# Moving five value products out of a graph layer's prologue, with GpSimd sharing the sort's ranks

## The chip, the cores and the metric

The kernel runs on one core of a Trainium2 chip. The metric is the device time in microseconds (us) of one execution, as a median of several. A profile is one further execution that the hardware profiler recorded.

## What is computed

One layer of a graph network over 1250 nodes of 512 features and 40000 edges, followed by a routed mixture of eight experts. Cut to what the change touches:

```python
xn = _layernorm(x, axis=-1)
xs = xn[:, :C] @ (W_in2f_s / np.sqrt(C))                # node table, with xv: 4 products of 128 features
sj, vj = xs[idx_j], xv[idx_j]                           # gathered for every edge
h = shifted_softplus(f_ij @ Wf1 + bf1)                  # filter network over the edges
W = (h @ Wf2 + bf2) * rcut_ij[:, None]
agg = segment_sum(x_ij, idx_i)                          # messages made of sj, vj and W, summed by node
q, k, v = xn @ Wq, xn @ Wk, xn @ Wv                     # q and k then softmax over each head
context = einsum('bhnd,bhne->bhde', k, v)
out = einsum('bhnd,bhde->bhne', q, context)
x = x + gnn + (out @ Wo + bo)
x = x + ffn(_layernorm(x))                              # top 2 of 8 experts
```

## The kernel before

The nodes form ten tiles of 125 rows (NB = 10, t below). The edges lie as 313 columns of 128 edges. The kernel has a prologue, a filter loop of 79 steps of four columns, a loop over gathered messages, and the experts. Each engine runs its own list of instructions in the order in which the code writes them; semaphores are the only link, so an engine that waits holds up all that is written behind the wait.

*Prologue.* SyncE (SP) loads x, the weights and the features. For each tile VectorE normalises (`normal`), TensorE transposes (`transpose_x`, L2058), ScalarE copies the transposed tile out (`evac_xT`, L1080), TensorE multiplies it with the table weights (`table_product`, L2070) and with Wv (`value_product`, L2081), and ScalarE copies both results (`table_rows`, L1085; `values`, L1092). All ten value products are in the prologue (L2091 and the following lines). SP stores each table tile.

*The sort.* Edges are to be stored in order of the receiving node. VectorE finds each edge's block of 125 nodes (`receiving_blocks`, L1400) and for each of the ten blocks a mask, a running count and a rank (`count_block`, L1411: mask, scan, copy of the last count, product, sum). TensorE sums the counts over the partitions, VectorE makes the bases of the blocks (`block_bases`, L1420) and the place of every edge (`places_in_blocks`, L1439, ten operations). GpSimd then makes the places of six spare columns (`spare_places`, L956) and scatters six empty records (`spare_record`, L938).

*The filter network* has weights that are split into a high and a low part. GpSimd orders them (L918 to L932), ScalarE rounds them, VectorE makes the low parts. Before the loop starts, the first columns must have gone through: features (`stage_f`, `stage_f_low`), TensorE's `transposes` and `layer1`, ScalarE's `radial` and `log_part`, VectorE's `hidden`, then `high` (ScalarE) and `low` (VectorE).

*The filter loop.* In step m TensorE multiplies four columns (`layer2`, L2227; the first instruction of a step is the bias product at L2240), ScalarE copies the first column out (`first_column`, L1202) and VectorE the other three (`column`, L1587), and GpSimd scatters four columns to their places in memory (`scatter`, L953). A ring of four steps holds the results, so that `stage` (L1555) waits for the scatter of four steps before. Beside this the steps carry the attention: from step 3 on, six steps make a group for one tile t (`beside`, L2247), with r = 0 to 5 the step in the group: the query product in r 0 and 1, the key product in r 2 and 3, the transposes of the queries in r 4, the context product in r 5. In the last steps of the first five groups (8, 14, 20, 26, 32) VectorE also runs `run_level` (L1446).

## Time and profile before

| | |
|---|---|
| median of 3 runs | 1272.28 us (1270.4 to 1272.28) |
| the profiled execution | 1271.56 us, span 1269.5 us |
| TensorE busy in the span | 1190.8 us (94%) |
| VectorE busy | 1071.0 us (84%) |
| GpSimd busy | 870.8 us (69%) |
| ScalarE busy | 812.4 us (64%) |
| prologue, until the first filter product | 75.2 us |
| filter loop, first to last start of a scatter | 79.5 to 493.7 us |

The profile page gives each engine's busy time, and groups of instructions by line with the idle time ahead of them and what ended it. The trace of the same execution can be asked for the chain of waits (the work that ended last, followed back), for timelines of one engine, and for stretches. Busy time of TensorE (PE) includes the overlap of pipelined products; PEld is its weight load. L12 is line 12 of the kernel. POOL is GpSimd, DVE is VectorE, ACT is ScalarE. A group such as "x8" in a timeline is so many instructions, and an fp32 product appears as two.

### The profile page before, as it was taken

What the parts mean: (1) busy time and instruction counts of PE and PEld (TensorE: products, weight loads), DVE (VectorE), ACT (ScalarE), POOL (GpSimd) and SP (SyncE); (2) the same over time, 40 slices, a digit from 0 to 9 for tenths busy, and PEclk for the clock granted to TensorE, in tenths of its full rate; (3) what the DMA queues carried; (4) which work ended last, traced back from release to release, by engine and by line L of the source; (5) the groups of instructions that cost most, each with busy time, mean ns of one, the idle gap of its engine ahead of it and who ended that gap; (6) DMA issues with size and microseconds to landing.
All of it is one profiled execution on the core that took longest, in us unless ns stands there. A gap on an engine that the chain in (4) does not pass through costs nothing.

```text
span 1269.5 us, 16249 instructions
## 1 busy us (share of the span) xinstructions
PE 1190.8 (94%) x4108; PEld 700.0 (55%) x4108; DVE 1071.0 (84%) x1998; ACT 812.4 (64%) x1822; POOL 870.8 (69%) x795
## 2 busy tenths in 40 slices
PE   4999999989999999899999999999999999977995
PEld 3566666767766664344444444444444444766882
DVE  5958999899989995699999999999999997589325
ACT  3667777777767660576776767767767674775330
POOL 6357777777777775688888888888888881053650
PEclk8989999999999999899999999999999999987996
DMA  9248876887799966988888898988898881554557
GB/s 276 63 153 298 296 266 256 314 304 270 291 320 358 305 236 233 351 302 309 316 309 307 305 315 305 311 309 302 315 309 304 310 265 34 203 188 143 183 172 235
DMA packets 106608, 337.65 MB, mean 266 GB/s; under 512 B 16783, under 2 KB 17803, under 8 KB 100373
## 3 DMA queue, kind: packets, MB, share of 16 engines
q0 software_dynamic: 57264, 188.75, 41.5%
q1 hardware_dynamic: 49252, 147.88, 35.4%
q8 instruction: 34, 0.56, 0.2%
q14 instruction: 58, 0.47, 0.1%
HBM read 211.27 MB, written 125.30 MB: 265 GB/s over the span
## 4 chain that ended last, share of the span: by engine, by line
PE 76%; DVE 12%; DMA 4%; issue 3%; ACT 2%; POOL 1%; SPq 0%; DVEq 0%; POOLq 0%; ACTq 0%
PE PS L2306 22%; PE PS L2311 22%; PE PS L2242 11%; PE PS L2431 6%; DVE RR L1587 4%; PE PS L2109 3%; PE PS L2119 2%; PE PS L2087 2%; DMA X<-in_x 1%; DMA edge_records<-RR 1%; DVE h_low L1580 1%; PE PS L2240 1%; PE PS L2409 1%; POOL edge_records L953 1%; PE PS L2202 1%
## 5 line engine op out<-in xcount | busy, mean ns | idle before, releaser
L990 POOL DMA_INDIRECT RR<-node_table,RR x322 | 445.4, 1383 | 112.2 <-issue 64.0
L1250 ACT ACTIVATE RR<-RR 128x256 f32<-128x256 f32 x966 | 394.5, 494 | 194.1 <-PE PS L2311 155.6
L953 POOL DMA_INDIRECT edge_records<-RR x316 | 315.0, 997 | 107.3 <-issue 72.7
L2306 PE MATMUL PS<-RR 128*125 128x512 f32 x644 | 291.6, 595 | 3.8 <-DVE RR L1765 3.7
L2311 PE MATMUL PS<-RR 128*125 128x512 f32 x644 | 289.6, 592 | 0.0
L2306 PEld LDWEIGHTS PS<-RR 128*125 128x125 f32 x644 | 121.0, 189 | 162.1 <-issue 144.4
L2311 PEld LDWEIGHTS PS<-RR 128*125 128x125 f32 x644 | 120.9, 188 | 155.5 <-issue 155.5
L1587 DVE TENSOR_TENSOR RR<-PS,RR 128x512 f32<-128x512 f32 x237 | 161.0, 687 | 23.4 <-PE PS L2242 22.7
L2242 PE MATMUL PS<-wf_high,h_high 128*128 128x512 f32 x316 | 148.5, 470 | 8.7 <-DVE RR L1587 8.4
L1765 DVE TENSOR_TENSOR RR<-RR 128x1536 f32<-128x1536 f32 (+1 forms) x81 | 141.0, 1741 | 0.0
L2242 PE MATMUL PS<-wf_low,h_high 128*128 128x512 f32 x316 | 125.9, 398 | 0.0
L2242 PE MATMUL PS<-wf_high,h_low 128*128 128x512 f32 x316 | 125.9, 398 | 0.0
L1736 DVE TENSOR_TENSOR RR<-RR 128x1024 f32<-128x1024 f32 (+1 forms) x81 | 98.2, 1213 | 21.6 <-DMA RR<-node_table,RR 21.5
L1748 DVE TENSOR_SCALAR RR<-iota_f,RR 128x125 f32<-128x125 f32 x322 | 109.6, 343 | 0.0
L1195 ACT ACTIVATE h_high<-RR 128x512 fp32r<-128x512 f32 x79 | 49.8, 630 | 55.1 <-PE PS L2242 52.0
L2242 PEld LDWEIGHTS PS<-wf_high,h_high 128*128 128x128 f32 x316 | 60.4, 191 | 27.6 <-DVE RR L1587 12.2
L1202 ACT ACTIVATE RR<-PS 128x512 f32<-128x512 f32 x79 | 47.2, 597 | 40.7 <-PE PS L2242 40.7
L1754 DVE TENSOR_TENSOR RR<-RR 128x512 f32<-128x512 f32 (+1 forms) x81 | 55.4, 684 | 20.4 <-ACT RR L1250 20.1
L2242 PEld LDWEIGHTS PS<-wf_low,h_high 128*128 128x128 f32 x316 | 60.7, 192 | 14.0 <-issue 9.1
L2242 PEld LDWEIGHTS PS<-wf_high,h_low 128*128 128x128 f32 x316 | 60.2, 190 | 14.2
L1785 DVE TENSOR_TENSOR RR<-RR,PS 125x1024 f32 x52 | 63.1, 1214 | 4.2 <-PE PS L2311 3.7
L1570 DVE SCALAR_TENSOR_TENSOR RR<-PS,RR 128x512 f32<-128x512 f32 x79 | 53.9, 683 | 9.5 <-ACT RR L1187 9.3
(354 smaller groups left out, 1799.1 us busy)
## 6 DMA issues: line engine op xcount, KB each, us to landing
RR<-edge_records SPq DMA_DIRECT2D x48, 1040.0 KB, 6.6
expert_inputs<-RR SPq DMA_DIRECT2D x8, 2313.0 KB, 17.7
RR<-edge_records SPq DMA_DIRECT2D x27, 520.0 KB, 5.1
RR<-edge_records SPq DMA_DIRECT2D x15, 780.0 KB, 5.5
RR<-in_L_ffn_beta_w SPq DMA_DIRECT2D x8, 1024.0 KB
expert_w_raw<-in_L_ffn_expert_w SPq DMA_DIRECT2D x8, 1024.0 KB, 7.0
RR<-edge_records SPq DMA_DIRECT2D x31, 260.0 KB, 5.2
edge_records<-RR POOLq DMA_INDIRECT x322, 4.3
```

The source lines that it names most:

```text
L953: g.indirect_dma_start(out=rec_dram, out_offset=place, in_=ST[:, j, :], in_offset=None).then_inc(scattered[c], 16)
L990: g.indirect_dma_start(out=GB[q % GBS][:, t, 1:5, :].rearrange("p k n -> p (k n)"), out_offset=None, in_=tab_dram, in_offset=bass.Indirect ...
L1250: last = a.activation(message_slot(q)[:, t, k:k + 5:4, :], GB[q % GBS][:, t, 0:k + 3:k + 2, :], ACT.Copy, scale=record_slot(q)[:, t, 4 * C ...
L1587: v.tensor_tensor(ST[:, c * STEP + j, 0:4 * C], PS[:, w_bank(m, j), :], b2_rows, ALU.add)\
L1736: v.tensor_tensor(gb[:, :, 0:2, :].rearrange("p t k n -> p k t n"), record_slot(q)[:, :, 0:2 * C].rearrange("p t (k n) -> p k t n", k=2), ...
L1748: v.tensor_scalar(OH[q % OHS][:, t, 0:NT], iota_f[:, 0:NT], rec[:, 3:4], rec[:, 5:6], ALU.is_equal, ALU.mult).then_inc(onehot, 1)
L1765: v.tensor_tensor(vec, vec, record_slot(q)[:, :, 2 * C:3 * C].unsqueeze(2).to_broadcast([P, n, 3, C]), ALU.mult).then_inc(d_ready, 1)
L1785: v.tensor_tensor(dst_ap, dst_ap, PS[0:NT, b:b + 2, :].rearrange("p b n -> p (b n)"), ALU.add)\
L2242: last = te.matmul(PS[:, w_bank(m, j), :], part[:, c % 2, edges], weights[:, :, :].rearrange("p k n -> p (k n)"), start=(j > 0 and weights ...
L2306: te.matmul(PS[0:NT, 2 * (r % PSS), :], OH[q % OHS][:, t, 0:NT], GB[q % GBS][:, t, 1:5, :].rearrange("p k n -> p (k n)"), start=(n == 0), ...
L2311: te.matmul(PS[0:NT, 2 * (r % PSS) + 1, :], OH[q % OHS][:, t, 0:NT], message_slot(q)[:, t, 0:4, :].rearrange("p k n -> p (k n)"), start=(n ...
L2431: last = te.matmul(PS[:, 2 + n % 2, :], x[:, n % 2, k, :], w[:, k, :], start=(j == 0), stop=(j == len(terms) - 1))
```

## The change

Value products 5 to 9 leave the prologue. Each becomes four quarters in the last step of a group t = 0 to 4 (`late_value`): two quarters behind the first column, one behind the second, one behind the fourth; its result goes through bank 6, which the queries use too, and ScalarE copies it at the head of the next step. As the memory of Wv is used again by then, Wv is loaded a second time. The first of the four quarters waits until ScalarE has copied the transposed queries out.

GpSimd makes the product and the sum of the ranks of blocks 0 to 7 (`rank_block`), in two buffers each, so VectorE's `count_block` waits from block 2 on for GpSimd's product of two blocks before; blocks 8 and 9 stay with VectorE. Five blocks stand ahead of the ordering of the filter weights on GpSimd, three behind it. Constants that GpSimd made early come behind the spare places. The six empty records are scattered in steps 1 to 6. The first batch of blank rows for the experts (`blank_words`) goes from step 3 to step 11.

SP issues the first filter layer's weights and the first features ahead of Wq and Wk. TensorE sums the counts after tile 4's transposes; tiles 5 to 9 use bank 6 for the transposes and bank 7 for the table. The first filter columns are interleaved with the table products of tiles 5 to 9. VectorE makes the places ahead of the first hidden layer. The inverse edge lengths are made early.

Buffers, groups and steps are renumbered; of the diff stands here what the order of the work depends on.

buffers, banks and steps:

```diff
+        running, block_product, own_ranks = (tA, tB), (tC, tD), (srcf, bkt)
...
+        WV_again = R1[:, sorted_at:sorted_at + KD * D].rearrange("p (k n) -> p k n", k=KD)
+        assert sorted_at + KD * D <= c1.at
...
+        FRONT = 5
...
+        EARLY_XT = 6
+        RANKED = 8
...
+        SPARE_STEPS = range(1, 1 + NCOL - LOOPED)
+        BLANK_STEP = [SPARE_STEPS[-1] + 5] + [2 * CHUNK * k + 2 for k in range(1, BLANKS)]
```

SyncE: loads:

```diff
-            load_projection(WQ, Wq, wqkv_in[0])
-            load_projection(WK, Wk, wqkv_in[1])
-            load_features(0)
-            load_features(1)
...
+            load_features(0)
+            load_projection(WQ, Wq, wqkv_in[0])
+            load_projection(WK, Wk, wqkv_in[1])
+            load_features(1)
...
+            sp.wait_ge(edge_places, 2)
+            load_projection(WV_again, Wv, wqkv_in[2])
```

GpSimd:

```diff
+            def rank_block(t):
+
+                pool.wait_ge(counts_ready, t + 1)
+                g.tensor_tensor(rnk if t == 0 else block_product[t % 2], block_mask[t], running[t % 2], ALU.mult)\
+                    .then_inc(ranked, 1)
+                pool.wait_ge(ranked, multiplied(t))
+                if t:
+                    g.tensor_tensor(rnk, rnk, block_product[t % 2], ALU.add).then_inc(ranked, 1)
+
+            for t in range(5):
+                rank_block(t)
...
+            for t in range(5, RANKED):
+                rank_block(t)
+
+            pool.wait_ge(nrm_inv, 1)
+            g.tensor_tensor(meta[:, 0:RC1, 0:3], rraw, inv.unsqueeze(2).to_broadcast([P, RC1, 3]), ALU.mult)\
+                .then_inc(dirs_ready, 1)
...
-            for n in range(NCOL - LOOPED):
-                spare_record(LOOPED + n)
...
+                if m in SPARE_STEPS:
+                    spare_record(LOOPED + SPARE_STEPS.index(m))
```

ScalarE:

```diff
+            table_rows(2)
+            evac_xT(3)
+            moments_of((6, 7))
+            later_std(slice(6, 8), 7)
+            values(2)
+            table_rows(3)
+            evac_xT(4)
+            rounded_weights()
+            stage_f(0)
+            stage_f(1)
+            moments_of((8, 9))
+            later_std(slice(8, NB), NB - 1)
+            a.preload_act_table_set("natural_log_exp_and_others")
+            values(3)
+            table_rows(4)
+            evac_xT(5)
+            act.wait_ge(w_ordered, 2)
+            a.activation(b2hl[0:2, :], b2f, ACT.Copy).then_inc(w_rounded, 1)
 
             def radial(i, c):
...
+                if r == 0 and 1 <= t <= NB - FRONT:
+                    values(FRONT + t - 1)
...
-            bias_rows()
-            table_rows(NB - 1)
             radial(0, 0)
             stage_f(2)
-            values(NB - 2)
+            table_rows(5)
+            evac_xT(6)
             log_part(0, 0)
             radial(0, 1)
+            stage_f(3)
+            values(4)
             high(0, 0)
-            stage_f(3)
-            values(NB - 1)
             log_part(0, 1)
+            table_rows(6)
+            evac_xT(7)
             radial(0, 2)
             stage_f(4)
+            bias_rows()
+            log_part(0, 2)
+            table_rows(7)
+            evac_xT(8)
             radial(0, 3)
-            log_part(0, 2)
+            table_rows(8)
+            evac_xT(9)
+            table_rows(9)
             for m in range(STEPS):
                 filters(m // RING, m % RING)
 
```

VectorE:

```diff
-                step(v.tensor_tensor_scan(tB, ones[:, 0:RC1], mask, 0.0, ALU.mult, ALU.add))
-                v.tensor_copy(cnt[:, t:t + 1], tB[:, RC1 - 1:RC1]).then_inc(counts_ready, 1)
-                step(v.tensor_tensor(tC, mask, tB, ALU.mult))
-                step(v.tensor_tensor(rnk, rnk, tC, ALU.add))
+                count = running[t % 2]
+                if t >= 2:
+                    dve.wait_ge(ranked, multiplied(min(t - 2, RANKED - 1)))
+                step(v.tensor_tensor_scan(count, ones[:, 0:RC1], mask, 0.0, ALU.mult, ALU.add))
+                v.tensor_copy(cnt[:, t:t + 1], count[:, RC1 - 1:RC1]).then_inc(counts_ready, 1)
+                if t >= RANKED:
+                    step(v.tensor_tensor(own_ranks[t - RANKED], mask, count, ALU.mult))
...
+                dve.wait_ge(ranked, multiplied(RANKED - 1) + 1)
+                for t in range(RANKED, NB):
+                    step(v.tensor_tensor(rnk, rnk, own_ranks[t - RANKED], ALU.add))
...
+            inverse_lengths()
             count_block(2)
             inverse_root(range(2, 4), 1)
             normal(2)
             normal(3)
             count_block(3)
+            count_block(4)
+            count_block(5)
             inverse_root(range(4, 6), 2)
             normal(4)
-            count_block(4)
             normal(5)
-            count_block(5)
-            count_block(6)
-            count_block(7)
-            inverse_root(range(6, NB), 3)
+            for t in range(EARLY_XT, NB):
+                count_block(t)
+            step(v.tensor_copy(meta[:, 0:RC1, 4].bitcast(I32), dsti))
+            dve.wait_ge(rcut_in, 32)
+            step(v.tensor_copy(meta[:, 0:RC1, 5], rcut))
+            block_bases()
+            inverse_root(range(6, 8), 3)
             normal(6)
-            count_block(8)
             normal(7)
-            count_block(9)
-            normal(8)
-            normal(9)
-            dve.wait_ge(w_rounded, 4)
+            dve.wait_ge(w_rounded, 3)
             stage_f_low(0, 0)
             stage_f_low(0, 1)
             for half_of in range(2):
...
                 last = v.scalar_tensor_tensor(wf1_parts[rows, half_of, :], wf1_parts[rows, half_of, :].bitcast(F32),
                                               wf1_sign[rows, :], wf1_low[rows, :], ALU.mult, ALU.add)
             last.then_inc(wf2_l, 1)
+            places_in_blocks()
+            inverse_root(range(8, NB), 4)
+            normal(8)
+            normal(9)
+            dve.wait_ge(w_rounded, 4)
             v.tensor_tensor(wf2_low[:, :, :], wf2[:, :, :], wf2_high[:, :, :].bitcast(F32), ALU.subtract)\
                 .then_inc(wf2_l, 1)
-            step(v.tensor_copy(meta[:, 0:RC1, 4].bitcast(I32), dsti))
-            dve.wait_ge(nrm_root, 1)
-            v.reciprocal(inv, inv).then_inc(nrm_inv, 1)
-            dve.wait_ge(rcut_in, 32)
-            step(v.tensor_copy(meta[:, 0:RC1, 5], rcut))
-            block_bases()
-            places_in_blocks()
 
             def stage(i, c):
 
                 cols = columns_of(i, c)
                 if real(i):
                     dve.wait_ge(scattered[c], i * (16 * STEP))
+                elif c == 2:
+                    dve.wait_ge(tab_psum, NB)
+                elif c == 3:
+                    for s in range(2):
+                        dve.wait_ge(tab_out[s], 32 * (NB // 2))
```

TensorE:

```diff
+            def late_value(t, k):
+
+                if t == FRONT and k == 0:
+                    pe.wait_ge(wqkv_in[2], 64)
+                if k == 0:
+                    pe.wait_ge(qT_ready, t - FRONT + 1)
+                last = te.matmul(PS[0:NT, value_bank(t), :], XTQ[:, t, k, :], WV_again[:, k, :], start=(k == 0),
+                                 stop=(k == KD - 1))
+                if k == KD - 1:
+                    last.then_inc(v_psum, 1)
+
+            table_product(0)
+            value_product(0)
+            table_product(1)
+            value_product(1)
+            transpose_x(2)
+            table_product(2)
+            transpose_x(3)
+            value_product(2)
+            table_product(3)
+            transpose_x(4)
+            block_counts()
+            value_product(3)
+            table_product(4)
+            transpose_x(5)
 
             def query(t, k):
                 if k == 0 and t == 0:
...
-            pe.wait_ge(w_rounded, 5)
-            te.matmul(PS[:, 5, :], ones2[:, :], b2hl[:, :], start=True, stop=True).then_inc(b2_psum, 1)
-            table_product(NB - 1)
+            pe.wait_ge(w_rounded, 1)
             transposes(0, 0)
-            value_product(NB - 2)
+            table_product(5)
+            transpose_x(6)
             pe.wait_ge(wf2_l, 1)
+            pe.wait_ge(xT_ready, EARLY_XT)
             layer1(0, 0)
             transposes(0, 1)
-            value_product(NB - 1)
-            pe.wait_ge(tab_ready, NB)
+            value_product(4)
+            pe.wait_ge(tab_ready, FRONT)
             layer1(0, 1)
+            table_product(6)
+            transpose_x(7)
             transposes(0, 2)
+            pe.wait_ge(w_rounded, 5)
+            pe.wait_ge(v_ready, FRONT - 1)
+            te.matmul(PS[:, 4, :], ones2[:, :], b2hl[:, :], start=True, stop=True).then_inc(b2_psum, 1)
             layer1(0, 2)
+            table_product(7)
+            transpose_x(8)
             transposes(0, 3)
+            table_product(8)
+            transpose_x(9)
+            table_product(9)
             pe.wait_ge(counts_read, 1)
-            pe.wait_ge(v_ready, NB)
-
+            pe.wait_ge(v_ready, FRONT)
             pe.wait_ge(b2_ready, 1)
             pe.wait_ge(wf2_l, 2)
 
...
                     key(t, 2 + j // 2)
                 elif 0 <= t < NB and r == 4 and j == 2:
...
-                elif 0 <= t < NB and r == PER - 1 and j == 2:
-                    context(t)
+                elif 0 <= t < NB and r == PER - 1:
+                    if j == 2:
+                        context(t)
+                    elif t < NB - FRONT:
+                        for k in ((0, 1), (2,), (), (3,))[j]:
+                            late_value(FRONT + t, k)
```

## Rows read from the trace of the kernel before

**Rows 1.** The page's first line.

```profile
span 1269.5 us, 16249 instructions
```

**Rows 2.** Chain of waits in order of time, 0 to 110 us: start, us, what.

```profile
4.06 18.97 DMA X<-in_x
...
42.45 3.44 PE PS L2087 x8
...
70.01 0.70 DVE RR L1570
```

**Rows 3.** TensorE's timeline, prologue: start, us, engine, line, operation, [idle before].

```profile
29.43 2.07 PE L2077 MATMUL PS<-RR 128*125 128x128 f32 x8 [0.95 <-ACT RR L1082]
...
36.20 1.04 PE L2077 MATMUL PS<-RR 128*125 128x128 f32 x8
...
75.17 0.73 PE L2240 MATMUL PS<-b_parts,ones_in_two_rows 128*128 128x512 f32 x1
```

**Rows 4.** GpSimd's timeline, prologue.

```profile
13.62 1.77 POOL L888 TENSOR_TENSOR RR<-RR 128x939 f32<-128x939 f32 x1
15.47 0.73 POOL L889 TENSOR_TENSOR RR<-RR 128x313 f32<-128x313 f32 x1
16.28 0.95 POOL L890 TENSOR_TENSOR RR<-RR 128x313 f32<-128x313 f32 x1
...
20.55 0.32 POOL L905 TENSOR_SCALAR_AFFINE_SELECT RR<-ones 128x128 f32<-128x128 f32 x1
...
31.22 0.61 POOL L920 TENSOR_SCALAR RR<-wf,small 128x128 f32<-128x128 f32 x1 [7.87 <-DMA wf<-in_L_gnn_bf]
...
34.94 0.77 POOL L928 TENSOR_SCALAR RR<-RR 2x128 f32<-2x128 f32 x1
```

**Rows 5.** VectorE's timeline, prologue.

```profile
13.34 2.24 DVE L1404 TENSOR_SCALAR RR<-RR 128x313 f32<-128x313 f32 x1
15.62 0.76 DVE L1405 TENSOR_SCALAR RR<-RR 128x313 f32<-128x313 f32 x1
...
27.70 0.32 DVE L1414 TENSOR_SCALAR RR<-RR 128x313 f32<-128x313 f32 x1
28.05 0.81 DVE L1415 TENSOR_TENSOR_SCAN RR<-ones,RR 128x313 f32<-128x313 f32 x1
...
28.97 0.47 DVE L1417 TENSOR_TENSOR RR<-RR 128x313 f32<-128x313 f32 x1
...
55.28 0.17 DVE L1423 TENSOR_SCALAR small<-PS 128x10 f32<-128x10 f32 x1
...
58.64 5.85 DVE L1442 SCALAR_TENSOR_TENSOR RR<-RR,small 128x313 f32<-128x313 f32 x10
```

**Rows 6.** ScalarE's timeline, the first logarithm and the next feature copy.

```profile
67.97 0.59 ACT L1183 ACTIVATE RR<-PS 128x512 f32<-128x512 f32 x1
...
69.89 0.37 ACT L1174 ACTIVATE fT<-PS 128x256 fp32r<-128x256 f32 x1
```

**Rows 7.** TensorE's timeline, steps 3 to 40: starts of steps, and waits.

```profile
92.92 0.39 PE L2240 MATMUL PS<-b_parts,ones_in_two_rows 128*128 128x512 f32 x1
...
181.75 0.50 PE L2242 MATMUL PS<-wf_high,h_high 128*128 128x512 f32 x1 [0.50 <-DVE RR L1587]
...
186.36 0.47 PE L2240 MATMUL PS<-b_parts,ones_in_two_rows 128*128 128x512 f32 x1 [1.14 <-DVE RR L1587]
...
248.19 0.47 PE L2240 MATMUL PS<-b_parts,ones_in_two_rows 128*128 128x512 f32 x1 [0.49 <-DVE RR L1587]
...
288.05 0.39 PE L2240 MATMUL PS<-b_parts,ones_in_two_rows 128*128 128x512 f32 x1
```

**Rows 8.** GpSimd: groups by shape, 91 to 498 us, and step 40's first scatter.

```profile
L953 POOL DMA_INDIRECT edge_records<-RR x308 | 307.3, 998 | 98.0 <-issue 71.8 <-DVE RR L1587 14.2 <-DVE RR L1560 9.4
...
291.74 0.97 POOL L953 DMA_INDIRECT edge_records<-RR  x1 [0.30 <-DVE RR L1560]
```

**Rows 9.** One stretch: us, busy us and count by engine, PEclk, DMA share, GB/s.

```profile
30.00:32.00 2.00, 2.00 (x12) 2.00 (x11) 0.22 (x2) 1.58 (x5) 0.78 (x2) 0.50 0.87 235
```

More of the change, by code:

```diff
@@ L968, in spare_places @@
                 step(g.tensor_copy(posi[REM:P, FULL:RC1], pd[REM:P, 0:1]))
-                g.tensor_copy(posi[:, RC1:NCOL], pd[:, 1:SPARE]).then_inc(places_ready, 1)
-                pool.wait_ge(places_ready, 1)
+                step(g.tensor_copy(posi[:, RC1:NCOL], pd[:, 1:SPARE]))
             spare_places()
+            g.affine_select(out=tie, in_=ones[:, 0:X8 * X8].rearrange("p (a b) -> p a b", b=X8), compare_op=ALU.is_gt,
+                            fill=0.0, base=0, pattern=[[1, X8], [-1, X8]], channel_multiplier=0)
+            g.iota(run_no, pattern=[[0, LEVELS], [1, MAXRUNS]], base=0, channel_multiplier=0,
+                   allow_small_or_imprecise_dtypes=True)
+            for z, size in enumerate(SIZES):
+                g.iota(run_tile[:, z, :], pattern=[[size, MAXRUNS]], base=0, channel_multiplier=0,
+                       allow_small_or_imprecise_dtypes=True)
+                g.memset(places_of[:, z, NB:NB + 1], float(NCOL - RUNS_OF[z] * size))
+            g.memset(ctxT[:, :, :].rearrange("p k n -> p (k n)"), 0.0)
+            g.memset(empty, 0.0).then_inc(empty_ready, 1)
             pool.wait_ge(empty_ready, 1)
-            for n in range(NCOL - LOOPED):
-                spare_record(LOOPED + n)
             pool.wait_ge(edge_places, 2)
@@ L1721, in _ @@
             stage_f_low(0, 4)
+            dve.wait_ge(b2_ready, 1)
             dve.wait_ge(dirs_ready, 1)
-            dve.wait_ge(v_psum, NB)
-            for s in range(2):
-                dve.wait_ge(tab_out[s], 32 * (NB // 2))
+            dve.wait_ge(v_psum, FRONT)
             stage(0, 0)
@@ L2130, in context @@
                 pe.wait_ge(k_norm, t + 1)
+                pe.wait_ge(v_ready, t + 1)
                 for k in range(KD):
```

121 lines of the change are left out of this document (48 added, 73 removed).

## The prediction

> **What bounds the kernel now.** I read the chain of waits first, then each engine's timeline up to 90 us, then the steps of the filter loop. The span is 1269.5 us inside a profiled run of 1271.56 us [rows 1]; the runs shown have a median of 1272.28, so the sum below stands on a run 0.7 us under the median.
>
> The change touches only the prologue and filter steps 1 to 32. The prologue's chain [rows 2] waits for the last x until 23.04, then is TensorE from 29.4 to 62: five tiles, each a table product, four transposes and a value product of 3.44 us [rows 2, 3]. From about 67 it leaves TensorE: ScalarE's logarithm (67.97 to 69.89, three operations) [rows 6], VectorE's first hidden layer at 70.01 [rows 2] and the feature copies decide, and the first filter product starts at 75.17 [rows 3]. Call that S0.
>
> In the loop two engines are nearly level. GpSimd issues four scatters a step; one takes 1.27 us from start to start (0.96 busy and 0.30 of issue) [rows 8], so 24 of them, six steps, need 30.4 us. TensorE takes from step 3 at 92.92 to step 33 at 248.19 [rows 7]: 155.3 us for five groups of six steps, 31.1 a group. So TensorE sets the pace of exactly the steps that get the value products. It is idle only at two places in each group's last step: 0.50 us ahead of the second column and 1.14 us ahead of the next step, both on VectorE [rows 7]; over the five groups these ten waits (0.49 to 1.15 each) make 7.4 us. At the end GpSimd still scatters until 495, but it follows TensorE: at step 40 it is only 3.7 us behind (288.05 and 291.74) [rows 7, 8], so from there everything shifts by what TensorE has shifted.
>
> **The change part by part.** *Value products.* Out of the prologue go five products of 3.44 us, 17.2 us of TensorE. They come back in steps 8, 14, 20, 26 and 32, the ones with the idle places. The first two quarters stand ahead of the 0.50 us wait and fill it; all four push the next step past the 1.14 us wait. 17.2 less 7.4 is +9.8; restarting after each of the ten waits also costs some 0.1 to 0.2 us which disappears, giving +7.9 to +9.8; the first quarter's new wait for ScalarE's copy of the queries (it ends about 0.2 us after that place is reached) takes some back. I take +8.4. ScalarE's five copies of 0.6 us move with them into steps that begin with a wait for TensorE; query products wait for them, but come 1.9 us into the step, so they cost nothing; if that cover is gone it is 0.6 us a group. The second load of the weights (1 MB on SP) waits for the last table row and the places, near S0, and is needed 40 us later: nothing.
>
> *Start of the loop.* I walk the queues with the old durations. x lands as before: it is ahead of the reordered loads on SP's queue, so the first 27.7 us stay. The filter weights, for which GpSimd now waits until 31.22 [rows 4], come earlier because SP issues them ahead of 2.6 MB of projections and features; but GpSimd now ranks five blocks ahead of using them.
> A block on VectorE loses its product and sum (0.47 and 0.49) [rows 5], 1 us of 2.3. GpSimd does both at some 0.85 us each (0.73 busy and 0.81 to the next start; 0.95 the longest) [rows 4]. It is free at 20.9, but block 3 can't be counted before VectorE has normalised tiles 2 and 3: its mask starts at 27.70 now as then [rows 5], and its scan and count are done at 28.9; blocks 3 and 4 end at 32.4. The weight ordering behind them keeps its 4.5 us (31.22 to 35.71) [rows 4]: 36.9. Then blocks 5 to 7: the product of block 7 is the fifth operation, 41.2. VectorE, which has counted block 6 by 34.2, stands in the wait that was added and counts block 9 only at 42.4 (the scan's 0.81 [rows 5] behind 41.2, and the copy).
> TensorE's block counts now wait for that, in line ahead of value product 3 and all that follows it: idle from 37.7 to 42.5. VectorE's bases (55.28 to 58.64 before, 3.4 us) [rows 5] then end near 46.7; two normalisations, the features and first weights 2.2: 48.9; two new sums 1.0; the places 5.85 [rows 5] and 0.4 of copies; two normalisations, the second weights and features 2.1; hidden layer 0.7: 58.9. The places formerly stood behind nothing urgent, now the hidden layer stands behind them.
> From there ScalarE sets the start, in its written order: first half 0.6, a logarithm 1.9, table and transposed tile 1.0, feature copies 0.5, bias rows 0.5, a logarithm 1.9, table, tile and features 1.3, then twice table product, copy, transpose, copy in turn with TensorE, which after its gaps works at half the clock: 0.50 granted between 30 and 32 us, when it had been without work until 27.4 [rows 9], that is 1.2 GHz, and a table product takes 2.07 instead of 1.04 us [rows 3]. That is 10.5 us at the high clock, 13 at the low one. I take 11.5.
> What is left is the port. A VectorE two-operand scaling took 2.24 us while GpSimd multiplied beside it from 13.62, the next one of the same shape 0.76 [rows 4, 5]. The new order has GpSimd computing during all of VectorE's later counting and during its bases. I add 1.5 us (0 to 4). S0 becomes 58.9 + 1.5 + 11.5 = 71.9, 3.3 us before the old 75.17; bounds 69.4 (no port waits, high clock but one) and 74.5.
>
> The Trainium skill, "SBUF — State Buffer", section "Who interferes with whom", says GpSimd and VectorE share one port pair as an exclusive lock, the second to issue blocked for the whole of the other's operation, two-input operations included. By that rule every count of blocks 6 to 9 and the bases would wait out a GpSimd operation, and the sum would be about 4 us higher. The 2.24 us row agrees.
>
> *First steps.* Step 0 to 3 take 17.75 us (75.17 to 92.92) [rows 3, 7]. Step 0 has a logarithm in ScalarE's way that is done earlier in the new order, and TensorE comes into it warmer: -0.7 (-1.35 to 0).
>
> *Scatters.* Six spare scatters of 1.27 us [rows 8] move from GpSimd's idle prologue into steps 1 to 6: 7.6 us on its queue. It then lags up to 9.6 us at step 8, and makes it up from 2.3 us of new slack a group (32.7 against 30.4); scattering alone would reach step 33 at S0 + 181, TensorE's pace brings it there at S0 + 185. VectorE's staging waits for the scatter four steps back, so a lag of about 9 plus slow landing could hold TensorE: +0.4 (0 to 2). The first batch of blank rows also moves from step 3 to step 11, next to the second. Constants that GpSimd now makes behind the spare places have 15 us of cover.
>
> Sum: -3.3 - 0.7 + 8.4 + 0.4 = **+4.8**, 1271.56 + 4.8 = **1276.4**. All low ends give -5.8 - 1.35 + 7.9 + 0 = +0.8, all high ends -0.7 + 0 + 9.8 + 2 = +11.1.
>
> **The rivals.** *The start follows TensorE (faster).* If the ranks and places don't hold up the hidden layer, the prologue shrinks by the removed 17.2 us and S0 is 58.0: 1271.56 - 17.2 - 0.7 + 8.4 + 0.4 = 1262.5. For it: TensorE is the chain from 29.4 to 62 [rows 2, 3], and every removed product lies in that stretch or just behind it. Against: the counts can't be complete before GpSimd is through, by operations that the rows price. It decides from S0 below 65.2; halfway, S0 at 65.0, gives 1269.5.
> *The port decides (slower still).* Some ten operations of VectorE (masks, scans and products of blocks 7 to 9, two copies, the bases) are each held for half of one of GpSimd's 0.85 us: +4 beyond my 1.5, 1280.4. For it the 2.24 us; against, the ten places of 5.85 us, no more than 0.59 each [rows 5], which ran beside GpSimd's spare places. The rule cited above is this case.
> *Scattering becomes the bound.* If the 7.6 us of spare scatters aren't absorbed, 1276.4 - 0.4 + 7.6 = 1283.6. Against: 2.3 us of slack in each of five groups.
> *The products cost nothing in the loop:* not possible beyond the 7.4 us of idle counted; TensorE has no other.
>
> **How the numbers follow.** Forecast 0.55 (of it 0.15 within 0.2%), the start following TensorE at least halfway 0.20, the port 0.17, scattering 0.08. A measurement of this kernel tells 0.2%, 2.5 us, from no change: the band is 1269.7 to 1274.8. Faster 0.2, same 0.2 (0.15, and 0.05 for a smaller part of the first rival), slower 0.6. The forecast's own bounds are 1272.3 to 1282.7. The range reaches down to 1267, into the first rival as far as S0 at 62.5, and up to 1283; that leaves out the rest of that rival (0.1) and the upper part of scattering (0.06).
>
> **What would show it.** The first filter product at 70 to 74; TensorE idle ahead of the block counts until about 42; VectorE waiting for GpSimd between blocks 6 and 9; hidden layer at 59 to 62; steps 8, 14, 20, 26, 32 of 7.9 to 8.2 us without waits on VectorE, and step 33 at S0 + 180. Wrong, if S0 is below 67, or if steps 3 to 33 take less than 160 us.

## The result: 1.0% slower, and the profile after

The changed kernel takes 1285.12 us (median of 4 runs, 1281.69 to 1287.91) against 1272.28, a ratio of 1.0103 with a 95% interval of 1.0076 to 1.0129. The prediction was 1276.4 (1267 to 1283): the sign was right, the size 8 us too small, and the time lies above the range.

The profiled run took 1284.5 us (its span is 1282.8), 12.94 more than the one of before. By the starts of the filter steps (the bias product, L2339 in this kernel, L2240 in before) the difference is made like this:

| stretch | before | after | difference | predicted |
|---|---|---|---|---|
| to the first filter product (S0) | 75.17 | 74.97 | -0.20 | -3.3 |
| step 0 to step 3 | 17.75 | 14.98 | -2.77 | -0.7 |
| step 3 to step 33, the products | 155.27 | 164.39 | +9.12 | +8.4 |
| step 3 to step 33, one stall in step 13 | | 5.11 | +5.11 | +0.4 |
| step 33 to step 78 | 228.02 | 227.67 | -0.35 | 0 |
| from step 78 to the end of the run | 795.35 | 797.38 | +2.03 | 0 |

The 164.39 is what steps 3 to 33 take in kernels with the products and without the stall (E1, E2, E9, E10 and E12 below: 164.38 to 164.41). The last line is no effect that I can place: over the kernels below the same stretch took 794.2 to 798.7 us with nothing in it changed.

TensorE's timeline (start, us, engine, line, operation, [idle before]), which answers to [rows 3, 7]:

```profile
46.58 0.60 PE L2161 MATMUL PS<-small,ltri 128*128 128x10 f32 x2 [8.59 <-DVE small L1478]
47.45 5.62 PE L2154 MATMUL PS<-RR 128*125 128x512 f32 x8
...
74.07 1.14 PE L2144 MATMUL PS<-RR 128*125 128x128 f32 x8 [0.72 <-ACT RR L1123]
74.97 0.48 PE L2339 MATMUL PS<-b_parts,ones_in_two_rows 128*128 128x512 f32 x1
...
143.71 0.40 PE L2339 MATMUL PS<-b_parts,ones_in_two_rows 128*128 128x512 f32 x1
...
147.26 0.80 PE L2341 MATMUL PS<-wf_high,h_high 128*128 128x512 f32 x1 [2.21 <-DVE RR L1656]
...
152.74 0.63 PE L2339 MATMUL PS<-b_parts,ones_in_two_rows 128*128 128x512 f32 x1
```

See that the block counts start at 46.58 after 8.59 us without work, and that step 13 (143.71 to 152.74) takes 9.03 us; in before it took 3.92.

VectorE, by groups from 18 to 47 us (count | busy us, mean ns | idle before and who ended it):

```profile
L1477 DVE TENSOR_TENSOR_SCAN RR<-ones,RR 128x313 f32<-128x313 f32 x10 | 11.8, 1183 | 3.0 <-POOL RR L939 2.7
L1473 DVE TENSOR_SCALAR RR<-RR 128x313 f32<-128x313 f32 x10 | 4.9, 488 | 0.0
```

The same groups of before, 18 to 47 us:

```profile
L1415 DVE TENSOR_TENSOR_SCAN RR<-ones,RR 128x313 f32<-128x313 f32 x10 | 8.2, 819 | 0.3
L1414 DVE TENSOR_SCALAR RR<-RR 128x313 f32<-128x313 f32 x10 | 3.5, 351 | 0.2
```

In before the ten scans took 8.2 us and the ten masks 3.5. VectorE gave up eight products and eight sums, 7.7 us at 0.47 and 0.49 each [rows 5], and got 3.6 us of longer scans, 1.4 of longer masks and 2.7 of waiting for GpSimd, 7.7 us together. Nothing is left. (GpSimd needed 14.2 us for the same work.) Not all of the 7.7 comes from the ranks: 1.5 us of it is the one scan that follows.

The cast of the nodes and the last scan of VectorE, and the GpSimd operation beside the scan, in the two timelines of after. That operation (L962) is no rank but the product that makes the edge directions; in before it ran at 55.01 us, behind the counting, and it now stands directly behind the ranks, since the inverse lengths are made early:

```profile
43.81 1.86 POOL L962 TENSOR_TENSOR RR<-RR 128x939 f32<-128x939 f32 x1
```

```profile
13.01 2.61 DVE L1462 CAST RR<-RR 128x313 f32<-128x313 int32 x1 [4.59 <-DMA RR<-in_dst]
...
44.06 2.27 DVE L1477 TENSOR_TENSOR_SCAN RR<-ones,RR 128x313 f32<-128x313 f32 x1
```

The scan begins 0.25 us after GpSimd's product, which ends at 45.67; the scan ends at 46.33, 0.66 later. It takes 0.81 alone [rows 5], so this one was 1.46 us longer.

### The profile page after: what moved, and what is told of

Read it like the earlier page. It is cut to its first block, busy times and chain, and to the rows that moved or that the text cites. A ratio compares the mean times of both kernels' runs of the same rounds, so it can differ in the third digit from the quotient of the medians.

```text
span 1282.8 us, 16276 instructions
## 1 busy us (share of the span) xinstructions
PE 1194.3 (93%) x4108; PEld 703.5 (55%) x4108; DVE 1070.0 (83%) x1982; ACT 813.1 (63%) x1823; POOL 870.4 (68%) x810
## 4 chain that ended last, share of the span: by engine, by line
PE 72%; DVE 11%; DMA 7%; issue 3%; POOL 3%; ACT 2%; SPq 1%; POOLq 0%; DVEq 0%; ACTq 0%
PE PS L2409 21%; PE PS L2414 21%; PE PS L2341 11%; PE PS L2534 6%; DMA edge_records<-RR 3%; DVE RR L1656 2%; PE PS L2196 2%; PE PS L2206 2%; POOL edge_records L985 1%; DMA X<-in_x 1%; PE PS L2170 1%; PE PS L2512 1%; PE PS L2339 1%; PE PS L2292 1%; DMA RR<-expert_outputs 1%
## 5 line engine op out<-in xcount | busy, mean ns | idle before, releaser
L1031 POOL DMA_INDIRECT RR<-node_table,RR x322 | 429.3, 1333 | 127.9 <-issue 69.9
L2341 PE MATMUL PS<-wf_high,h_high 128*128 128x512 f32 x316 | 148.3, 469 | 10.6 <-DVE RR L1656 10.1
L1649 DVE TENSOR_TENSOR h_low<-RR,h_high 128x512 fp32r<-128x512 f32 x79 | 54.3, 687 | 9.4 <-ACT h_high L1241 9.4
```

The lines of the kernel that those rows point to most:

```text
L1031: g.indirect_dma_start(out=GB[q % GBS][:, t, 1:5, :].rearrange("p k n -> p (k n)"), out_offset=None, in_=tab_dram, in_offset=bass.Indirect ...
L2341: last = te.matmul(PS[:, w_bank(m, j), :], part[:, c % 2, edges], weights[:, :, :].rearrange("p k n -> p (k n)"), start=(j > 0 and weights ...
```

## The experiments

All are edits of the changed kernel, except where before is named; each ratio is to runs of before in the same series. X is the time from the first product S0 to step 3.

| | S0 | X | step 13 | step 33 - step 3 | step 78 at | median us | ratio to before (95%) |
|---|---|---|---|---|---|---|---|
| before | 75.17 | 17.75 | 3.92 | 155.27 | 476.21 | 1272.28 | |
| after | 74.97 | 14.98 | 9.03 | 169.50 | 487.12 | 1285.12 | 1.0076 to 1.0129 |
| E1 spare scatters ahead | 74.74 | 17.94 | 3.92 | 164.39 | 484.65 | 1279.3 | 1.0027 to 1.0065 |
| E2 and first blank rows at step 3 | 74.06 | 14.98 | 3.92 | 164.39 | 480.85 | 1279.42 | 1.0031 to 1.0085 |
| E3 counts later | 75.96 | 16.38 | 3.92 | 165.56 | 485.43 | 1282.29 | 1.0055 to 1.0109 |
| E4 places later | 74.33 | 17.60 | 3.92 | 165.42 | 485.34 | 1281.76 | 1.0038 to 1.0084 |
| E5 both later | 72.05 | 14.98 | 5.87 | 166.59 | 480.80 | 1279.49 | 1.0035 to 1.0075 |
| E6 ranks back | 73.33 | 14.98 | 5.79 | 166.34 | 482.44 | 1283.71 | 1.0058 to 1.0113 |
| E7 half of the late products | 74.85 | 14.98 | 8.25 | 161.01 | 479.45 | 1277.72 | 1.0008 to 1.0039 |
| E8 before, spare scatters in the steps | 75.04 | 18.07 | 6.09 | 158.60 | 479.85 | 1275.01 | 1.0000 to 1.0032 |
| E9 E2 and E5 | 72.02 | 14.98 | 3.92 | 164.41 | 478.67 | 1278.83 | 1.0019 to 1.0051 |
| E10 E9 and ranks back | 74.16 | 14.99 | 3.92 | 164.38 | 480.89 | 1278.81 | 1.0030 to 1.0057 |
| E11 E10, reordered | 65.27 | 14.99 | 3.92 | 169.79 | 477.28 | 1274.92 | 0.9999 to 1.0027 |
| E12 E11, bases early | 65.55 | 16.55 | 3.92 | 164.41 | 473.50 | 1271.13 | 0.9979 to 1.0008 |

Whole runs of one kernel spread over 4 to 10 us in most series (one run of E11 took 3132 us; without it the median is 1274.51), so the readings below go by the steps. Each kernel was profiled once, so how far its own steps spread is not known; between kernels, steps 3 to 33 agree within 0.03 us where nothing in them differs. S0 is less sure. ScalarE's wait for x (22.45 us in after) ends between 21.98 and 23.72 us in the profiles of after and of the experiments, and S0 moves with it: from that moment to S0 it is 52.5 us in after and 51.8 to 52.5 in E1, E2 and E7, whose TensorE, VectorE and ScalarE do the same up to S0. Differences in S0 of about 1 us therefore tell nothing.

### The stall: lag and landing (E1, E2, E8)

```diff
             pool.wait_ge(empty_ready, 1)
+            for c in range(LOOPED, NCOL):
+                spare_record(c)
             pool.wait_ge(edge_places, 2)
             for m in range(STEPS):
                 scatter(m // RING, m % RING)
-                if m in SPARE_STEPS:
-                    spare_record(LOOPED + SPARE_STEPS.index(m))
```

> After, with the six spare scatters back ahead of the loop; the first blank rows stay at step 11. Theory L (lag): the spare scatters in steps 1 to 6 put GpSimd's scattering some 8 to 13 us behind, and the 5.1 us by which step 13 was too long (9.03 us against 3.92) is this lag reaching VectorE's staging copy, which waits for the scatters of the chunk before. Then the lag at step 8 falls from 12.8 us to under 6, step 13 takes 3.9 to 4.2 us, and the time falls by 4 to 6 us, to about 1280. Rival B (burst): the step is late because two bursts of blank rows (the one moved to step 11 and the one of step 14) stand in the transfer queues at once, ahead of the scatters; then the lag falls just the same but step 13 still takes 7 to 9 us, and the time falls by 0 to 2 us.

E2 has also `BLANK_STEP = [TILE_STEP] + ...`:

> After, with the spare scatters ahead of the loop and the first blank rows back at step 3. Theory L: as with the spare scatters alone, about 1280; the blank rows' step adds nothing (within 1 us of that run). Rival B: only now does step 13 fall to 3.9 to 4.2 us, and the time to about 1280, 4 to 5 us under the run with the spare scatters alone. If neither of the two runs takes the 5.1 us away, both theories fall.

E8 (before, with one spare scatter in each of steps 1 to 6 and `BLANK_STEP = [11] + ...`):

> Before, with nothing changed but the spare scatters, one each in steps 1 to 6, and the first blank rows at step 11. Theory L (lag): without any of the products in the loop GpSimd's lag rises to 9 to 13 us at step 8 all the same, step 13 takes 6 to 9 us in place of 3.9, and the time rises by 2 to 5 us. Rival W (the lag bites only together with the second load of the value weights, which stands in the queues at 77 us and on, or with the longer steps): the lag rises, but step 13 stays under 4.5 us and the time within 1 us of before.

In E1 the lag of GpSimd behind TensorE at step 8 falls from 12.8 us to 5.2, and step 13 takes 3.92 us. E2 keeps that (lag 6.0). E8, without any product in the loop, has a lag of 11.3 us, and step 13 takes 6.09 (VectorE waited 2.82 us for the landing of edge records). Theory L holds; the stall is smaller without the products, 3.3 us between steps 3 and 33 against 5.1. E8 begins step 78 3.6 us later than before; its time rises by 0.16%, 2 us, which its interval (1.0000 to 1.0032) only just tells from nothing.

What L lacks is why the stall comes in step 13, when the lag had been 9.5 to 12.8 us in all of steps 7 to 13. The transfers of after show it. Issues of transfers, first from 118 to 132 us, then from 135 to 147 (how many, median us from issue to landing):

```profile
edge_records<-RR POOLq DMA_INDIRECT x11, 2.7
...
edge_records<-RR POOLq DMA_INDIRECT x10, 9.4
```

From 135.06 us on SyncE puts two bursts of blank rows into the queues; SyncE's timeline:

```profile
135.06 0.33 SPq L728 DMA_DIRECT2D expert_inputs<-RR  x1
135.43 0.62 SPq L729 DMA_DIRECT2D expert_inputs<-RR  x1
...
138.99 1.28 SPq L728 DMA_DIRECT2D expert_inputs<-RR  x1
140.31 1.36 SPq L729 DMA_DIRECT2D expert_inputs<-RR  x1
```

VectorE's staging copy of after, the wait that stops step 13:

```profile
146.27 0.28 DVE L1629 COPY RR<-RR 128x32 f32<-128x32 f32 x1 [4.14 <-DMA edge_records<-RR]
```

A lag of 10 us with a landing of 2.7 us stops nothing (steps 8 to 12 of after). The same bursts without the lag stop nothing (E1). Both together do: the four steps that the ring gives, 21.2 us from step 9 to step 13, are shorter than lag, four scatters and a landing of 9.4 us. Nor does it take two bursts: E11, below, stalls in step 5 with a lag of 12.7 us and one burst, at a median landing of 7.6 us. And the slow landing isn't new: in before, where only the second of the two bursts falls there (issued from 133.41 us; the first went at 94.05), the median from 133 to 145 us is already 8.6 us, and VectorE doesn't wait for it, with a lag of 4.4 to 5.0 us in steps 9 to 13. What the burst moved to step 11 adds is not shown: no run has the spare scatters in the steps and the first blank rows at step 3.

Of the 5.11 us only 2.21 are TensorE's wait; the rest comes behind it, while the granted clock is 0.50, that is 1.2 GHz. E5 and E6, below, have the same lag (9.5 to 10.1 us in steps 9 to 13) and the same bursts. In E5 VectorE's wait for the landing was 2.61 us instead of 4.14, TensorE waited 0.67 and 0.78 us in step 13, the clock stayed at 1.00, and the step took 5.87 us:

```profile
142.82 0.50 PE L2341 MATMUL PS<-wf_high,h_high 128*128 128x512 f32 x1 [0.67 <-DVE RR L1655]
...
144.74 0.50 PE L2341 MATMUL PS<-wf_high,h_high 128*128 128x512 f32 x1 [0.78 <-DVE RR L1655]
```

With a third wait of 0.43 us in step 14 E5's waits make 1.9 us, and its steps 3 to 33 are 2.2 us longer than without a stall. In after a wait of 2.21 makes them 5.11 longer: 2.9 us of that go with the clock, and whether it falls differs between kernels with the same lag. Stretches of after (us, TensorE busy, weight load, VectorE, ScalarE, GpSimd, PEclk, DMA share, GB/s):

```profile
143.00:147.00 4.00, 2.05 (x10) 1.50 (x8) 0.73 (x3) 1.00 (x3) 3.00 (x4) 0.99 1.02 367
147.00:150.00 3.00, 2.74 (x7) 2.22 (x8) 2.96 (x6) 1.89 (x5) 2.39 (x3) 0.50 1.06 316
150.00:153.00 3.00, 3.00 (x10) 2.41 (x10) 2.87 (x8) 1.92 (x4) 2.30 (x3) 0.50 1.03 399
```

### The start of the loop: two engines at once (E3, E4, E5)

E3 moves `block_counts()` on TensorE behind `transpose_x(5)`. E4 moves the places on VectorE:

```diff
             last.then_inc(wf2_l, 1)
-            places_in_blocks()
...
             stage_f_low(0, 4)
+            places_in_blocks()
             dve.wait_ge(b2_ready, 1)
```

> After, with VectorE's places (twelve instructions, 5.8 us, from 55.2 to 61.0 us) moved behind the first hidden layers, into the 5.1 us in which VectorE waited for ScalarE at 71 us. Theory V: the first filter product (74.97 us) hangs on VectorE, whose places stand ahead of the last two normalised tiles and the first hidden layer: the hidden layer comes at 57 to 58 us in place of 63.2, the last normalised tiles 5 to 6 us earlier, and the first product falls by 3 to 5 us, to 70 to 72; the time falls as much, less what the first scatter gives back if the places now end after 77 us. Rival T: the start hangs on TensorE's and ScalarE's chain of transposes, evacuations and table products: the hidden layer comes earlier, but the first product stays at 74 to 75.5, and so does the time.

> The same, and TensorE's block counts moved behind the value product 3, table product 4 and transposes 5, so that TensorE doesn't stand idle for 8.6 us (to 46.6 us) ahead of them. Theory V: 0 to 1 us more than with the places alone, since TensorE isn't what is late; the bases come 1 to 8 us later, which costs nothing as long as the places end before 76 us. Rival T (TensorE's chain sets the start): the value product 3 begins at 38 to 40 us in place of 47.45, and the first product falls by 3 to 6 us more, to 66 to 70.

> After, with only TensorE's block counts moved behind transposes 5 (the places stay where they are on VectorE). It completes the square: after 74.97, places later alone 74.33, both 72.05. Theory B (both engines are late at the start, and either alone keeps it where it is): the first filter product at 74 to 75 us, since VectorE's places still hold the hidden layer at 61 us and later. Rival T (TensorE's idle 8.6 us were the whole cause, and the places did nothing): the first product at 72 to 72.5 us, as with both.

Either edit alone leaves S0 within 1 us of where it was (75.96 and 74.33 against 74.97), both together bring 72.05, and 72.02 in E9, which has both too. Counted from the end of ScalarE's wait for x it is 52.3 (E3), 51.6 (E4), 49.9 (E5) and 49.4 us (E9), against 52.5. (E3 and E4 have the stall one step later, 9.03 and 8.88 us in step 14 in place of 7.9, so what they gain on after is the smaller stall and not the start. E5 lies between its two theories, 2.3 us under E4.) So E4's theory V, which I had held in the prediction too, falls: VectorE's places weren't the one thing that the start waited for. With the places gone TensorE, which stood idle until 46.6 and then made its value product mostly at half the clock (5.62 us at a granted 0.65, against 3.60 in E5), was as late; with the counts gone, the places were. E3's theory B holds, with S0 1 us above what it had named; x came 1.2 us later in that profile.

### The ranks (E6, E10)

```diff
-                if t >= RANKED:
-                    step(v.tensor_tensor(own_ranks[t - RANKED], mask, count, ALU.mult))
+                step(v.tensor_tensor(rnk if t == 0 else block_product[0], mask, count, ALU.mult))
+                if t:
+                    step(v.tensor_tensor(rnk, rnk, block_product[0], ALU.add))
```

with the waits for `ranked` and GpSimd's `rank_block` calls taken out.

> After, with the products and sums of the ranks of all ten blocks back on VectorE, right behind each scan, and none on GpSimd. Theory P (the two engines hinder each other): on VectorE alone a product takes 0.47 us and a sum 0.49 us, 8.2 us for eight blocks; in after, the scans, masks and copies beside GpSimd are longer by about as much and VectorE waits 2.7 us for GpSimd. Then the counts are complete at 46 to 49 us (46.6 in after), the first filter product stays within 2 us of 74.97, and the time within 2 us of after. Rival H (the help is real): the counts come 7 to 9 us later, at 53 to 56 us, the first filter product at 79 to 83, and the time 4 to 8 us above after.

> After, with the places behind the first hidden layers, the block counts behind transposes 5, the spare scatters ahead of the loop, the first blank rows at step 3, and the ranks all on VectorE. Theory P: with the places and counts out of the way what sets the start is GpSimd (its ranks put the second bias row's correction at 45 to 48.7 us, and TensorE stands idle for it until 52.9), so without ranks the first filter product falls from 72.05 to 66 to 69 us, and the time is 3 to 6 us below that of the kernel with the same edits and ranks on GpSimd: 1268 to 1273, about that of before. Rival C: the chain of ScalarE sets the start, and the first filter product stays at 71 to 73; then 1273 to 1277, above before.

E6: TensorE's counts and the first filter product, timeline:

```profile
47.12 0.60 PE L2153 MATMUL PS<-small,ltri 128*128 128x10 f32 x2 [9.28 <-DVE small L1472]
...
73.33 0.48 PE L2331 MATMUL PS<-b_parts,ones_in_two_rows 128*128 128x512 f32 x1
```

VectorE, 18 to 47 us, by groups:

```profile
L1471 DVE TENSOR_TENSOR_SCAN RR<-ones,RR 128x313 f32<-128x313 f32 x10 | 10.1, 1011 | 0.3
L1473 DVE TENSOR_TENSOR RR<-RR 128x313 f32<-128x313 f32 x10 | 5.7, 570 | 0.0
```

VectorE does all ten products and nine sums and is only 0.54 us later with the counts (47.12 against 46.58); S0 is 1.64 us earlier, of which 1.0 are the two sums ahead of the places, which are gone. ScalarE's wait for x ended at the same time in both (22.43 and 22.45). GpSimd's help was worth half a microsecond of counting. Theory P holds, though the eight blocks that it prices at 8.2 us make 7.7 by its own 0.47 and 0.49. (The 10.1 us of scans are nine of 0.81 and one of 2.82, beside the product of the edge directions.) E10's expectation fails: S0 is 74.16, not 66 to 69, and 2.1 us behind E9, the same kernel with the ranks on GpSimd. Of these, 1.1 us stand in the landing of x (ScalarE's wait for it ended at 23.72 us, 22.65 in E9); so with the places and counts out of the way the help may be worth about 1 us. One scan took 2.82 us beside GpSimd's product of the edge directions, and TensorE's first feature transposes came at 54.11: they wait for VectorE's feature parts, which stand behind the counts and the bases. E11 goes on from that.

### The price of the products in the loop (E7)

```diff
-                last = te.matmul(PS[0:NT, value_bank(t), :], XTQ[:, t, k, :], WV_again[:, k, :], start=(k == 0),
-                                 stop=(k == KD - 1))
+                if k not in (0, KD - 1):
+                    return
+                last = te.matmul(PS[0:NT, value_bank(t), :], XTQ[:, t, k, :], WV_again[:, k, :], start=True,
+                                 stop=True)
```

> After, with the value products of tiles 5 to 9 cut to two of four matmuls each, each complete by itself, so that half of the work of these five products is left out. Theory T (TensorE's own time is the price of the products in the loop): the five steps with r = 5, now 7.85 to 7.92 us against 6.28 to 6.47 before, fall by 0.7 to 0.9 us each, and step 33 comes 3.5 to 5 us earlier against step 3 (besides what becomes of the stall of step 13). Rival E: the steps are longer through the extra evacuation on ScalarE and its wait, or through the clock; then they fall by under 0.4 us each.

The five steps fall by 1.35 to 1.64 us (7.91 to 6.48, 7.88 to 6.29, 7.84 to 6.20, 7.86 to 6.29, 7.85 to 6.50). That is about twice what theory T said and nearly all of the 1.72 us removed (half of a product of 3.44 [rows 2]). The expectation had halved the net price; but the idle time of 1.64 us in such a step [rows 7] hides the first half whichever half is left, so the second half is paid in full. E7 still makes the five copies, so in these steps the cause is TensorE's time, not the copies.

### A version that undoes the losses (E9, E11, E12)

> The same four edits with the ranks left on GpSimd as in after. If the start and the stall add up: first filter product at 72.05, as with the places and counts alone; step 13 of 3.9 us; step 40 at 289 to 291.5 us and the time 1274 to 1277. If they don't add up (the earlier start ends in another wait), step 40 stays at 292 to 294 and the time at 1278 to 1280.

E9: S0 and the stall add up, as expected (step 40 at 289.97), but the median of 1278.83 lies above the 1274 to 1277 that went with it; the profiled run, from which the steps are read, took 1275.43. It still begins step 78 2.5 us later than before.

E11 keeps E10's edits and reorders VectorE so that the first filter columns don't stand behind the sort; its code in the new order:

```python
             count_block(6)
             inverse_root(range(6, 8), 3)
             normal(6)
             dve.wait_ge(w_rounded, 3)
             stage_f_low(0, 0)
             weight_parts()
             normal(7)
             stage_f_low(0, 1)
...
             count_block(7)
             count_block(8)
             count_block(9)
...
             hidden(0, 1)
             block_bases()
             stage_f_low(0, 4)
             places_in_blocks()
```

and TensorE's `block_counts()` behind `value_product(4)`.

> The kernel with all four edits and the ranks on VectorE, reordered once more: the normalised tiles 6 and 7, the first feature parts and both weight parts stand ahead of blocks 7 to 9 on VectorE, the block bases behind the second hidden layer, and TensorE's block counts behind value product 4. Theory O (the order of VectorE sets the start): TensorE's first feature transposes, at 52.9 to 54.1 us in the two kernels before, come at 44 to 47 us, ScalarE has the first hidden layer's input 5 to 8 us earlier, and the first filter product falls from 72 to 74 to 65 to 69 us; all else as with the four edits, so that step 78 begins at 472 to 476 us and the time is 1269 to 1273, at or below that of before. Rival C (the chain through ScalarE or the landing of X sets it): the first product stays at 70.5 to 74 and the time at 1275 to 1279.

TensorE's first feature transposes come at 43.87, S0 at 65.27, 9.7 us before after. But GpSimd's first scatter came 11.3 us behind it, and step 5 took 10.22 us in place of 4.80, so step 78 (477.28) and the time (1274.92) miss what theory O had named. E12 moves the bases up behind the first hidden layer, and GpSimd's constants ahead of the spare places:

> The reordered kernel, in which the first filter product came at 65.3 us but GpSimd's first scatter only at 76.6 and step 5 took 10.2 us in place of 4.8, with the block bases moved up behind the first hidden layer (to 55 to 58 us in place of 57.8 to 60.2) and GpSimd's constants (66 to 68.5 us there) ahead of the spare places. Theory L (lag): the first scatter comes at 70 to 71.5 us, 5 to 6 us behind the first product; step 5 takes 4.8 to 6 us, nothing else changes, step 78 begins at 472 to 474 us and the time is 1268.5 to 1271.5, 0.2 to 0.4% under before. Rival S (the scatters' total work, and not when it begins, sets the steps): the 5 us come back as a longer step at 6 to 14, step 78 stays at 476 to 478 and the time at 1273 to 1276.

TensorE's and GpSimd's timelines of E12, the first filter product and the first scatter of edges:

```profile
44.74 0.41 PE L2278 MATMUL PS<-ident_rounded,feature_columns 128*128 128x128 f32 x2 [2.88 <-issue]
...
65.55 0.48 PE L2336 MATMUL PS<-b_parts,ones_in_two_rows 128*128 128x512 f32 x1
```

```profile
72.62 0.96 POOL L981 DMA_INDIRECT edge_records<-RR  x1 [0.30 <-ACT RR L1244]
```

The lag is 7.1 us at step 0 and 5.7 at step 5, and step 5 takes 4.80 us again: theory L holds, with the first scatter 1.1 us behind the 71.5 us that it had named. Step 78 begins at 473.50, 13.6 us before after and 2.7 before before. The time, 1271.13, is 14 us under after; against before (1273.05 in the same series) the interval of 0.9979 to 1.0008 doesn't tell it from no change. The 9.6 us that the start gains on before are about what the products cost in the loop.

## Why the prediction was right in sign and wrong in size

*Start of the loop, -3.3 predicted, -0.2 found.* The failed step is the term "what is left is the port. I add 1.5 us (0 to 4)". The walk had TensorE's counts at 42.5 without it; TensorE got them at 46.58, so 4.1 us went into the counting alone, the upper bound of the term, and 0.8 more behind it (hidden layer's end at 63.84, 17.3 us after the counts, 16.5 in the walk). Of the 4.1 us, 1.5 are the last scan, beside the product of the edge directions; that the change moves this product up there, the walk had left out. ScalarE's part, 11.5 us, was right (63.84 to 74.97 is 11.1). The row that I had weighed (2.24 us for 0.76 [rows 5]) was one of the pattern, not an exception; in after it is the cast of the nodes that took 2.61 us, against 0.43 in before. (That is no price of the change: the GpSimd products beside it stand in both kernels and hold now one operation, now the next.) The Trainium skill, "SBUF — State Buffer", section "Who interferes with whom", says that whichever of VectorE and GpSimd takes the shared ports first keeps them for its whole instruction and the other is blocked. The trace agrees: the scan of 44.06 waited out GpSimd's product to 45.67. The 2.24 us row shows less, since there VectorE's operation starts 0.28 us before GpSimd's [rows 4, 5]. So the rival "the port decides" was the case, and its +4 near the price (S0 is 3.1 us over the sum's 71.9); I had given it 0.17. The upper bound of 74.5 for S0 was also too low by the walk's own terms: 58.9, 4 for the port and 13 for ScalarE at the low clock make 75.9.

The other half of this step, "VectorE's places stand ahead of the hidden layer", was right as a fact and wrong as the cause: E3 to E5 show two chains of about equal length. A saving in one of them alone moves S0 by no more than the profiles differ anyway.

*First steps, -0.7 predicted, -2.77 found.* The term was named ("TensorE comes into it warmer") and undersized. It is the granted clock: 1.00 over all of 74.97 to 89.95 in after, against 0.78 and 0.67 in steps 0 and 2 of before. The stretch of after, then steps 0 and 2 of before:

```profile
74.97:89.95 14.98, 14.98 (x98) 12.92 (x97) 10.20 (x28) 10.21 (x21) 9.34 (x10) 1.00 0.66 240
```

```profile
75.17:81.24 6.07, 6.07 (x31) 4.94 (x31) 3.34 (x7) 5.70 (x12) 1.42 (x2) 0.78 0.05 18
...
87.77:92.92 5.15, 5.15 (x21) 4.20 (x19) 2.99 (x10) 2.94 (x6) 2.28 (x3) 0.67 0.39 151
```

It isn't a steady gain of the change: E1, whose TensorE has the same instructions, has 0.53 in step 2 and X of 17.94. Both have a slow stretch ahead of S0 (0.50 from 68 to 71 us), so that doesn't tell them apart; why the clock falls in one and not in the other stays open. X is 14.98 or 14.99 us in eight of the twelve changed kernels, so part of the gain of 2.77 us is luck. Step 2 of E1:

```profile
86.41:92.68 6.27, 6.27 (x20) 5.13 (x18) 3.18 (x10) 2.93 (x6) 2.72 (x3) 0.53 0.41 140
```

*Value products, +8.4 (7.9 to 9.8) predicted, +9.12 found.* Right, mechanism and size: the waits are filled (no wait for VectorE is left in step 20), and E7 prices the rest. 7.90 of it lie in the five steps named, of 7.8 to 7.9 us each (7.9 to 8.2 forecast); 1.28 lie in four steps behind them (5.59 for 5.27 each). There the prediction had said that the query products' wait for ScalarE's copies costs nothing, or 0.6 us a group if its cover is gone; found are 0.3. In E7, which has the copies too, these steps take 5.26 to 5.53, so the copies alone don't explain them.

*Scatters, +0.4 (0 to 2) predicted, +5.11 found.* The lag was forecast (9.6 us at step 8, 12.8 found) and its danger named, "a lag of about 9 plus slow landing could hold TensorE". The failed step is the size of this term: I let the lag be made up before anything happened to it, and put no number on the landing. The landing was there to be read in before, 8.6 us in the median beside the second burst of blank rows; with the lag still at 9.5 to 10.1 us in steps 9 to 13, VectorE waited 4.14 us and TensorE 2.21, and the fall of the clock behind that wait, which the prediction didn't have at all, brought it to 5.11.

*Scattering as the bound* and *start follows TensorE* didn't come: GpSimd's lag is 3.0 us again at step 15, and S0 stayed above 65.2. E11 and E12 come to 65.3 and 65.6, not to that rival's 58.0, with the ranks back on VectorE and another order.

The range failed because two misses came together: the port at its upper end (+3.1 against the sum) and the stall beyond its bound (+4.7). The first steps took 2.1 us of this back, and the end of the run, which I can't place, added 2.0.

## What to carry to other kernels

Handing elementwise work from VectorE to GpSimd can lengthen what stays on VectorE by as much as it takes away, where both run on such operations at the same time: here 7.7 us were given away and 7.7 lost, and the help was worth 0.5 us of counting (E6), perhaps 1 us where the rest of the start was out of the way (E10). Look also at what else moves up beside the helped engine: the longest hold came from an operation that had not been handed over. When a queue that has slack is given a backlog, look for the next burst of transfers before the backlog is made up: the stall is lag plus landing, and neither alone shows it. Where two engines are equally late, test them together: single edits say "no effect" of both. And where one profile stands for each kernel, find an event that should not differ, such as the landing of x, and see how far it does.

## What the runs showed of the hardware that was not expected

- A short wait costs more than itself: in after 2.21 us of idle TensorE in step 13, and 2.9 us more while the granted clock was 0.50 from 147 to 153 us; in E5 two waits of 0.67 and 0.78 us left it at 1.00.
- The granted clock in the first three steps differs between kernels whose TensorE runs the same instructions, by 3 us (X of 14.98 in after and E2, 17.94 in E1).
- The landing of GpSimd's scattered records goes from 2.7 to 9.4 us, though each transfer is as small as before, while SyncE's blank rows are in flight; in before, with one burst in flight there, it is 8.6 us.
- Two scans of 128x313, 0.81 us alone, took 2.27 us (after) and 2.82 us (E6) beside GpSimd's product of 128x939, and both ended 0.66 or 0.67 us behind it.
